# A four-layer graph network on one core: 98 groups instead of 99, the difference stage with operands in PSUM, and the node table built inside the dense stage

## What is computed

```python
h = jnp.maximum(_layernorm(x), 0.0)
# layer 0, typed attention: q, k, v by node type, score per edge, softmax over the edges of a destination
score = jnp.sum(qW[etype, dst] * k[src], axis=-1)
x = x + _typed_matmul(segment_sum(alpha[:, None] * vW[etype, src], dst), W_out, node_type)
# layer 1, differences along edges
cosim = relu((h_src * h_dst / scale) @ proj_cosim)
gate = exp(clip(cosim.sum(-1, keepdims=True), -5.0, 5.0))
src_diff = segment_sum(h_src - h_dst, dst)
h_diff = segment_sum(src_diff[src] * gate, dst)
x = x + relu(h_diff @ W_ffn.T + b_ffn)
# layer 2: agg = segment_sum(h[src], dst); x = x + (relu((h + agg) @ W0 + b0) @ W1 + b1)
# layer 3: attention with 4 heads, output projection and a second layernorm
```

## Time and profile before

| what | us |
|---|---|
| median of three runs | 6134.51 |
| lowest and highest run | 6123.38, 6164.55 |
| the profiled execution | 6107.96 |
| its span | 6106.2 |
| busy: PE, DVE, POOL, ACT | 4672.7, 4451.1, 3711.2, 2457.3 |

### The profile page before, as it was taken

The page is one execution under the profiler, slowest core; times in us unless marked ns, Lnnn a source line. Parts: engine busy times, 40 slices in busy tenths (PEclk is TensorE's granted clock), DMA queues, the critical chain, the costliest instruction groups (busy, mean ns, idle before and its releaser), DMA issues. The chain is left out here.

```text
span 6106.2 us, 72677 instructions
## 1 busy us (share of the span) xinstructions
PE 4672.7 (77%) x18059; PEld 2558.0 (42%) x18059; DVE 4451.1 (73%) x7915; ACT 2457.3 (40%) x7345; POOL 3711.2 (61%) x3983
## 2 busy tenths in 40 slices
PE   0577766779999978999788866555887777777876
PEld 0455544534444435666444432222333334444443
DVE  5688876778888879999766656665776756666666
ACT  0677765634444433555333322221232333333333
POOL 1566655466666630000488878886777667777777
PEclk9999987889999989999755555555778866777666
DMA  9333334434443439999533324444555522222221
GB/s 354 114 111 105 112 116 120 121 82 90 88 91 81 91 60 249 285 286 285 141 83 84 84 71 111 109 109 97 144 146 144 137 72 66 63 65 65 64 60 40
DMA packets 841646, 732.35 MB, mean 120 GB/s; under 512 B 541164, under 2 KB 548290, under 8 KB 841104
## 3 DMA queue, kind: packets, MB, share of 16 engines
q1 hardware_dynamic: 539184, 518.43, 29.6%
q0 software_dynamic: 102464, 90.84, 8.9%
q10 hardware_dynamic: 199584, 118.45, 6.4%
HBM read 454.79 MB, written 276.55 MB: 120 GB/s over the span
## 5 line engine op out<-in xcount | busy, mean ns | idle before, releaser
L1373 POOL DMA_INDIRECT df_hs<-u,keep_idx x396 | 503.2, 1271 | 832.3 <-POOLq L243 708.3
L887 POOL DMA_INDIRECT sc_xg<-t,keep_gather x396 | 439.2, 1109 | 312.9 <-DVE sc_h L196 139.1
L800 POOL DMA_INDIRECT t<-keep_ptr_pay,keep_scat_ptr x396 | 397.7, 1004 | 358.6 <-POOLq L243 125.8
L1373 POOL DMA_INDIRECT hd_gat<-u,keep_idx x396 | 478.3, 1208 | 160.6 <-issue 118.0
L1906 POOL DMA_INDIRECT out_x<-hd_x,keep_scat_out x396 | 457.2, 1154 | 150.1 <-issue 119.3
L1373 POOL DMA_INDIRECT ml_gat<-u,keep_idx x396 | 403.1, 1018 | 156.1 <-issue 68.9
L1373 POOL DMA_INDIRECT pr_gat<-sd,keep_idxsd x396 | 412.4, 1042 | 111.0 <-issue 72.2
L1362 PE MATMUL at_ps_m<-at_vx,keep_msg_twice 128*128 128x512 f32 x792 | 363.6, 602 | 23.2 <-DVE at_vx L1253 23.2
L1056 PE MATMUL sc_ps_r<-sc_qx,keep_weights 128*64 128x512 f32 x792 | 361.2, 599 | 10.6 <-DVE sc_prod L968 10.6
L2046 PE MATMUL hd_ps_h<-keep_weights,hd_xb 128*128 128x128 f32 x792 | 249.4, 415 | 134.1 <-DVE hd_wn L1989 121.3
L679 ACT ACTIVATE den_dh<-den_dc,den_dn_rstd 128x64 f32<-128x64 f32 x1188 | 303.8, 335 | 78.0 <-issue 50.5
(11 more groups left out here) (315 smaller groups left out, 12790.5 us busy)
## 6 DMA issues: line engine op xcount, KB each, us to landing
u<-den_dh SPq DMA_DIRECT2D x198, 256.0 KB
t<-tab_row ACTq DMA_DIRECT2D x99, 272.0 KB, 11.2
tab_x<-in_x SPq DMA_DIRECT2D x99, 256.0 KB
den_dx<-in_x SPq DMA_DIRECT2D x99, 256.0 KB
out_x<-den_dx SPq DMA_DIRECT2D x99, 256.0 KB
sc_et<-in_etype_row SPq DMA_DIRECT2D x99, 256.0 KB
at_v<-vt SPq DMA_DIRECT2D x198, 128.0 KB
at_et<-in_etype_row SPq DMA_DIRECT2D x99, 256.0 KB
```

The source lines that it names most:

```text
L800: pool.indirect_dma_start(pairs, bass.IndirectOffsetOnAxis(ap=e.scat_ptr[:, c:c + 1], axis=0), e.ptr_pay[:, c, :], None, bounds_check=NP * ...
L887: pool.indirect_dma_start(xg[i][:, u, :], None, e.T0, bass.IndirectOffsetOnAxis(ap=e.gather0[:, b.n, u:u + 1], axis=0), bounds_check=NP - ...
L1373: pool.indirect_dma_start(gat[i][:, u, :], None, table, bass.IndirectOffsetOnAxis(ap=idx_all[:, c:c + 1], axis=0), bounds_check=rows - 1, ...
```

## The change

1. `NG` becomes 98, the fewest groups that hold all edges, for edges and nodes. Waits that had `NG // U` count the groups of their slot instead.
2. `tables` no longer builds `T0`. The four `exact_thirds` follow the other small operations at once. The node types stay in a tile `e.ntypes` that is kept.
3. `dense` builds `T0`. There are 14 slots `row`. SP loads the features straight into the 68-wide rows, 14 node groups at step 0 and 7 at each later step until all 98 are issued, and holds for the slot to be written out. POOL clears columns 64 to 67 once, copies the types in and issues the write to `T0` itself. When all writes have landed it begins with the scatters of the pointers, now from step 18 on (six per step as before).
4. `EARLY` goes from 48 to 20, so 20 groups are gathered in `dense` and 78 are in `LATE`. Each of these 20 also holds for a value of `x2_done` that rises from step 84 to the last. SP stores them from step 87 on.
5. In `difference`, `lastv` becomes `ps_l` in PSUM, `diff` is written over `ps_t` in PSUM, and the order of the five DVE operations is new. PE puts `prod` in as the weights, so that `ps_p` has edges on partitions, and ACT takes the relu with an accumulating output straight into `gate`. The ones matmul, the relu tile and the copy go.

```diff
-NG = -(-EDGES // (GE * U)) * U
+NG = -(-EDGES // GE)
-EARLY = 48
+EARLY = 20
@@ tables @@
-                sp.dma_start(types[:, :], node_type).then_inc(types_in, 16)
-
-                def body(st):
-                    if st.on():
-                        wait(sp, copied, st.n - (UT - 1), e.sp_passed)
-                        sp.dma_start(xin[st.s][:, :, :], node_rows(e.x, st.n * GN)).then_inc(x_in[st.s], 16)
-                run_groups(sp, body, UT, 0)
+                sp.dma_start(e.ntypes[:, :], node_type).then_inc(types_in, 16)
+                wait(sp, types_in, 16, e.sp_passed)
...
-                        act.dma_start(node_rows(e.T0, st.n * GN), row[st.s][:, :, :]).then_inc(row_out[st.s], 16)
...
-                        v.tensor_copy(row[st.s][:, :, 0:D], xin[st.s][:, :, :]).then_inc(copied, 1)
-                        v.tensor_copy(row[st.s][:, :, D], types[:, bass.ds(st.n * RN, RN)]).then_inc(typed, 1)
-                    if st.n in thirds:
-                        exact_thirds(*thirds[st.n])
-                run_groups(v, body, UT, 0)
+                exact_thirds(e.bias_h, 0, e.bfo_cent[:, :])
+                exact_thirds(e.bias_h, 1, e.bfo_beta[:, :])
+                exact_thirds(e.bias_m, 0, e.W["b1_row"])
+                exact_thirds(e.bias_m, 1, b1_cent[:, :])
@@ dense @@
-        head = count * 71 // 99
+        UT = 14
+        row = [s.sb(f"row{i}", [P, RN, TW]) for i in range(UT)]
...
+        def rows_at(n):
+            return range(0, UT) if n == 0 else range(min(NG, UT + 7 * (n - 1)), min(NG, UT + 7 * n))
+        head = count * 88 // 99
...
-                PACE = 6
+                for i in range(UT):
+                    pool.memset(row[i][:, :, D:TW], 0.0).then_inc(cleared, 1)
+                wait(pool, cleared, UT, e.pool_passed)
+                for n in range(NG):
+                    i = n % UT
+                    wait(pool, row_in[i], 16 * (n // UT + 1), e.pool_passed)
+                    pool.tensor_copy(row[i][:, :, D], e.ntypes[:, n * RN:(n + 1) * RN]).then_inc(typed, 1)
+                    wait(pool, typed, n + 1, e.pool_passed)
+                    pool.dma_start(node_rows(e.T0, n * GN), row[i][:, :, :]).then_inc(row_out[i], 16)
+                for i in range(UT):
+                    wait(pool, row_out[i], 16 * len(range(i, NG, UT)), e.pool_passed)
+                PACE, START = 6, 18
                 for c in range(CH):
                     if c % PACE == 0:
-                        wait(pool, den.x2_done, c // PACE, e.pool_passed)
+                        wait(pool, den.x2_done, START + c // PACE, e.pool_passed)
...
+                first = START - (-CH // PACE)
                 for k, b in enumerate(early):
                     i = k % XU
                     wait(pool, xd_out[i], 16 * (k // XU), e.pool_passed)
+                    wait(pool, den.x2_done, first + (count - first) * k // len(early), e.pool_passed)
...
                     den.sync(sp, den.step(n))
+                    for r in rows_at(n):
+                        wait(sp, row_out[r % UT], 16 * (r // UT), e.sp_passed)
+                        sp.dma_start(row[r % UT][:, :, 0:D], node_rows(e.x, r * GN)).then_inc(row_in[r % UT], 16)
@@ difference, DVE, in the new order @@
+                        v.wait_ge(hb_done, b.n + 1)
+                        v.tensor_tensor(prod[b.s][:, :], ps_t[b.s][:, :], hb[b.s][:, :], ALU.mult).then_inc(prod_done, 1)
...
-                        v.scalar_tensor_tensor(out=lastv[:, :], in0=same[i][:, :], scalar=-1.0, in1=hd[i][:, :],
+                        v.scalar_tensor_tensor(out=ps_l[:, :], in0=same[i][:, :], scalar=-1.0, in1=hd[i][:, :],
...
-                        v.tensor_tensor(diff[:, :], ps_t[b.s][:, :], hb[b.s][:, :], ALU.subtract).then_inc(diff_done, 1)
+                        v.tensor_tensor(ps_t[b.s][:, :], ps_t[b.s][:, :], hb[b.s][:, :], ALU.subtract).then_inc(diff_done, 1)
...
+                        v.tensor_tensor_scan(hb[i][:, ::-1], same[i][:, ::-1], ps_l[:, ::-1],
...
-                        v.tensor_tensor_scan(sd[b.s][:, ::-1], same[b.s][:, ::-1], diff[:, ::-1],
+                        v.tensor_tensor_scan(sd[b.s][:, ::-1], same[b.s][:, ::-1], ps_t[b.s][:, ::-1],
@@ difference, ACT and PE @@
-                        a.activation(act[:, :], ps_p[:, :], ACT.Relu).then_inc(relu_done, 1)
...
-                        a.copy(e.gate[:, bass.ds(pos(b) * TU, TU)], ps_c[:, :]).then_inc(c_kept, 1)
+                        for u in range(TU):
+                            c = pos(b) * TU + u
+                            m = a.activation(junk_p[:, u, :], ps_p[:, u, :], ACT.Relu, accum_out=e.gate[:, c:c + 1])
+                        m.then_inc(c_kept, 1)
...
-                        pe.matmul(ps_p[:, :], e.W["proj"][0:D, :], prod[b.s][:, :], start=True, stop=True).then_inc(p_ready, 1)
+                        for u in range(TU):
+                            m = pe.matmul(ps_p[:, u, :], prod[b.s][:, u * P:(u + 1) * P], e.W["proj"][0:D, :],
+                                          start=(u == 0), stop=(u == TU - 1), skip_group_check=True)
```

87 lines of the change are left out of this document (27 added, 60 removed).

## The result

The changed kernel takes 6098.99 us (median of 10 runs, 6074.67 to 6113.76) against 6136.26 us for the kernel before in the same comparison (10 runs, 6122.43 to 6164.55). The ratio is 0.9937, with a 95% interval of 0.992 to 0.9954. The forecast was 5926 us with a range of 5840 to 6035, so it was wrong: a gain of 0.6% where 3.4% was forecast. The profiled execution took 6074.67 us, with a span of 6072.4 us.

The account below looks back on a forecast made before the run. Each stage has its own limit: DMA in tables, DVE in dense and attend, PE in scores, POOL in difference. Terms sum to -209 us, span 6106.2 to 5897, forecast 5926 us; range for 8 in 10 5840 to 6035.

Parts of the forecast that it names:

- tables: Stage tables: without the 99 row loads, copies and stores, its successor starts at 55.2 us instead of 166.9, -112 us.
- table build in dense, first 13 steps: Start of dense: DVE follows the DMAs that build the table, 226 us against 129, +96 us (+70 to +140).
- rest of dense: Dense from step 13 to the last x2: 71 steps at 9.67 us, 13 at 10.3, -77 us (-95 to -55).
- scores: Stage scores: 28 more groups gathered, POOL narrowly takes over from PE, +22 us (+60 or +5 as other cases).
- difference: Stage difference: PSUM operands cut gathers from 1.27 to about 1.02 us, 5.3 us per group, -107 us.
- one group less elsewhere: Attend, propagate, mlp and heads: 3147 us for 99 groups and about four steps of fill, -31 us.
- PSUM does not free the gathers: Rival in difference: groups keep 6.3 us, +101 us, total 6027 us; chance 7%.
- scores becomes POOL's with longer gathers: Rival in scores: gathers at 1.25 us each, 98 groups take 1091 us, +88 more, total 6014 us; chance 9%.
- The prediction's own sign of error: Wrong if dense's first 13 steps take 400 us or more, scores grows over 100 us, or difference's gathers stay above 1.2 us.

Follow-up runs that it names:

- set 5: Runs on one chip without long waits: kernel before 5837.0 us, changed kernel 5679.3 (0.9725), 128x16 memset in scores 5716.5, all memsets 128x16 5665.7.
- set 4: Changed kernel without dense's scatters, plain DMAs for gathers of scores and difference: 5674.0 us; with only scores' source gathers replaced and consecutive rows in difference: 5894.8 us.

## Why the prediction was wrong

The terms of the sum, with the two sides that can be told apart now: the first comparison (long waits) and set 5 (none).

| term | forecast | first comparison | set 5 |
|---|---|---|---|
| tables | -112 | -118 | -117 |
| table build in dense, first 13 steps | +96 | +69 | +85 |
| rest of dense | -77 | -70 | -12 |
| scores | +22 | +151 | +35 |
| difference | -107 | -35 | -113 |
| one group less elsewhere | -31 | -31 | -32 |
| sum | -209 | -34 | -154 |

The last two columns come from the stages' first instructions and from the steps of `x2`, so their sums are off by up to 2 us.

**Tables** was right in mechanism and size: `x2` of the first group starts at 51.6 us, its load at 48.9 (55.2 forecast). Its four thirds, 3.81 us each in the earlier trace rows, are 15.2 us and not 15.4, which changes nothing.

**The table inside dense** was right in mechanism: the DMA share is 1.12 at 322 GB/s in the first 199 us, and DVE follows the DMAs. It was too dear: step 13 comes 196 us after the first and not 226, and +69 lies just under its bounds of +70 to +140. The price of the row load was taken from a row of small pieces in `scores`, 1.22 us. The 0.89 us that the prediction weighed and set aside makes the same sum 194 us. The windows of dense in the kernel after, to step 13, to step 84, and to the last `x2`:

```profile
48.90:247.50 198.60, 108.40 (x456) 73.31 (x456) 88.31 (x172) 91.60 (x258) 76.92 (x210) 0.78 1.12 322
247.50:930.00 682.50, 507.54 (x2819) 369.61 (x2820) 575.29 (x1137) 523.99 (x1555) 400.84 (x398) 0.94 0.34 112
930.00:1075.00 145.00, 103.07 (x519) 72.99 (x518) 105.55 (x207) 96.58 (x285) 76.84 (x74) 0.84 0.47 129
```

**The rest of dense** was right here by its numbers (828 us from step 13 to the last `x2`, 821 forecast), and set 5 shows what it was made of: there the steps of before take 9.1 us up to the last, and nothing is to be won by spreading the gathers. The -70 was relief from the long waits, all of it but some 12 us.

**The failed step is that of scores**: "PE's pattern is ... 10.02 us now, some 9.85 without hiccups. So POOL takes over from PE, narrowly. With 15 us for the hiccups ...". It treated POOL as a queue: as long as its gathers fit into the group, they cost nothing. Set 5 is that world, and there the term was +35, near enough to 22: 97 intervals of 10.07 us against 10.13 forecast for POOL. In the first comparison POOL's gathers did something else. From 600 of them POOL went to 704, the runs between two pauses over 1 us grew from 12 gathers to 24 in the median (4 to 52), and PE's results reached ACT and DVE 3 to 13 us late. The hiccups of 15 us became some 150. That the transfers make them is shown by set 4, and that these 28 groups' gathers do by the run with EARLY = 48 (1054 us with 592 gathers, 1220 with 704 on the same chip). Their number in a step matters: with 9, 7 and 6 scatters a step the steps are 16.2, 13.0 and 9.7 to 10.3 us, with none 9.0, on chips that have the long waits. That the length of the run matters is not shown: 1220 us in scores came with runs of 12 in the median, and before's `difference` with 396 in one run has no long waits.

The evidence was in the rows. The prediction itself says of the last third of dense that "the steps are 2 us longer while the work is the same" and that they "began with the long runs". It used this for a gain in dense, where transfers were taken away, and not for a loss in scores, where they were added.

**Difference** was right in its mechanism, the gathers at 1.065 us for 1.02, and where there are no long waits in size too: 529.7 us for 533. (Of the three operations that it names only the two scans changed: the subtraction had `ps_t` in PSUM before.) Its step that failed is the same one: "Four with their gaps take 5.3 us". They do, but with the faster gathers the long waits come into a stage that had none with the slower ones, and take back 72 us of 107. The rule of the Trainium skill that was weighed there (SBUF — State Buffer, "Who interferes with whom": a DVE operation with two SBUF inputs contends with a GpSimd operation that reads SBUF), which by the prediction's estimate would have made a group 6.15 us, came close in the number (6.10) and not in the cause. In set 5 a group takes 5.3 us with the same two-input operation in it.

**One group less** was right.

**The rivals.** Of the five, "PSUM does not free the gathers" at 6027 us and "scores becomes POOL's with longer gathers" at 6014 us are nearest in time, both with the wrong mechanism: the gathers of difference fell to 1.07 us, and those of scores stayed at 1.10. None had the lateness of signals. The range held 5840 to 6035 and the result lies 64 us above it. The range covered how dear each known cost is, and had no room for a known symptom with an unknown cause. The prediction's own sign of error, scores growing by over 100 us, is the one that came.

## What to carry to other kernels

- When moving gathers or scatters onto a stage where POOL "has room", look not only at its busy share but at whether the trace already shows long waits of ACT and DVE on PE's results ("remote", or with a releaser of another stage) in the stages where POOL gathers. Where it does, count the transfers of a step: six scatters in a step of 9 us cost 0.7 to 1.3 us, seven cost 4, nine cost 7. Where it doesn't, six cost nothing. Memsets between the transfers helped in one stage of three where they were tried on such chips.
- A symptom that is used for a gain in one stage must be priced in every stage that gets more of it.
- A change that trades DMA or DVE time for denser GpSimd transfers has to be timed on several chips: this one is worth 0.6% on one and 2.8% on another, and EARLY = 34, the better number by POOL's rate, was 1% slower than before.
